# v's projection and the output projection change places in the batch loop of a graph-attention kernel

## The chip, the cores and the metric

The kernel runs on one core of one Trainium2 chip. The metric is the device time of one execution in microseconds. A core has five engines that run their own instruction queues and meet through semaphores: TensorE (PE, its weight loads shown as PEld), VectorE (DVE), ScalarE (ACT), GpSimd (POOL), and SyncE (SP), which here only issues DMAs. An engine carries out its queue in order, so whatever stands behind a waiting instruction waits too.

## The reference

For each of 32 graphs with 256 nodes and 512 features, with 16 heads of 32 features, in float32:

```python
h = jnp.maximum(_layernorm(x, axis=-1), 0.0)
q, k, v = h @ Wq.T, h @ Wk.T, h @ Wv.T            # split into 16 heads of 32
a = einsum('bhnd,bhmd->bhnm', q, k) * 512 ** -0.5 + (adj + adj)[:, None]
row_nonzero = jnp.any(a != 0, axis=-1, keepdims=True)
p = softmax(where(row_nonzero, a, -inf)); p = where(isnan(p), 0.0, p)
o = einsum('bhnm,bhmd->bhnd', p, v)               # heads joined again
out = x + o @ Wo.T
```

## The kernel before

**Precision.** Float32 products are made of float16 ones: every operand is split into a high and a low part (`*_hi`, `*_lo`), and three products (high-high, high-low, low-high) are added in PSUM. ScalarE evicts a PSUM bank into the high part, VectorE then takes the rest into the low part and frees the bank. Both have to be done before the bank is used again.

**Slots and steps.** One slot handles three batches at once: the batch before (`prev`), the current one (`cur`) and the next (`nxt`). A slot has 16 steps, one for each head of the current batch; `slot(t)` of each engine writes out by hand what it does in which step. There are 34 slots: `first`, `second`, 30 in the steady loop, `last` and `tail`. In a slot TensorE projects q, k and v of the next batch and the output of the batch before, computes the scores of four heads at a time (steps 0, 4, 8, 12), and multiplies probabilities by v (also in steps 0, 4, 8, 12, for the four heads of two groups earlier).

**Projections.** `JOBS` names eight jobs of two steps each: q01 in steps 0 and 1, q23, k01, k23, then o0 and o1 (steps 8 to 11), then v0 and v1 (12 to 15). Each job fills one of two PSUM banks, alternately; `pj_taken[0]` and `pj_taken[1]` count how often a bank was freed, `pj_full` how many jobs are done. So each job waits until the one two places before it has left the bank. q, k and v jobs are followed by an eviction on ScalarE one step later (`take_q`, `take_k`, `take_v`; v in steps 14 and 0) and the rest on VectorE another step later (`take_qk`, `take_v`; v in 15 and 1). The output jobs are followed only by `residual` on VectorE (steps 10 and 12, L759), which scales, adds x and writes the sum over x in SBUF. Job o0 waits for `o_split` (L953's group, in step 8): GpSimd must have split all four groups of o of the batch before, the last of them in its step 7.

**Softmax.** VectorE's `logit_rows` (L669) adds the adjacency to the scores and finds the row minima, two blocks of rows per head; ScalarE takes the exponential two steps ahead of its step number (L488) and rounds the head before that to float16 (L501); GpSimd's `split_probs` (L394) takes the rest; SyncE issues the DMA transpose of that head one step later (L325), and TensorE multiplies with v when four heads have landed. VectorE's `invert` (steps 3, 7, 11, 15: a reciprocal, L686, and `some`, L687) gives the factors that GpSimd spreads (`norm`, L403, one step later) and TensorE turns (L999). VectorE's `take_norm` copies them (L706), `take_o` (L698) applies them, and GpSimd's `take_o` (L413 and L416, in steps 3, 7, 11, 15) splits the result. `some` reads two SBUF tensors; L669, L698, L721, L731 and L759 read one from PSUM and one from SBUF.

**Next batches.** VectorE takes the statistics of the batch after next in steps 0 and 2 (L574, L580, L582, L583), GpSimd normalises in step 3 (L368, L374 `xn`), TensorE turns h in steps 5 and 9 (L836). `test_rows` (step 14 of VectorE, L745 and L753) tests rows for zeros. x has a ring of five buffers; its load is issued in SyncE's step 2, the two halves of the output are stored in SyncE's steps 12 and 14, each after its residual, and the load of a buffer waits for the store from it.

**Wo.** The weights are split at the start; Wo's four chunks are turned in steps 7 to 10 of the second slot (`WO_STEP`, L874), when that slot has no output projection and the two banks are free. v0 and v1 of that slot wait for two of the chunks to be taken from the banks.

Of the kernel before, what the change touches and what calls it, by code (L numbers as in the profile page):

```python
# [8 lines left out]
ALU = mybir.AluOpType  # L9
# [25 lines left out]

JOBS = ("q01", "q23", "k01", "k23", "o0", "o1", "v0", "v1")
NJ = len(JOBS)


class Slot:  # L40
# [23 lines left out]
    def uses(self, j):  # L64

        return self.prev if j in (4, 5) else self.nxt


def emit(nc, x_d, adj_d, wq_d, wk_d, wv_d, wo_d, out_d):
# [5 lines left out]
    with ctx:  # L75
# [162 lines left out]
        def full_step(t, j):  # L238
            if t.nxt:
                return 3 if j == 3 and not t.prev else 1  # L240
            return {4: 5, 5: 3}[j]

        def taken_step(t, j):
            if t.nxt:
                return 2 if j in (2, 3) and not t.prev else 1
            return 4

        def bank_free_at(t, j):

            return pj_taken_at(t, j) - (1 if t.nxt else 3)  # L250

# [5 lines left out]
        def group(t, c):  # L257

            d = c // NC
            return (d, c % NC) if t.has(d) else (None, None)  # L260

        def later(t, d):
# [12 lines left out]

        WO_STEP = 7

# [25 lines left out]
        def _(sp):  # L303
# [24 lines left out]
            def slot(t):  # L328
                for s in range(H):
                    turn(t, s - 1)  # L330
                    if s == 0 and later(t, 2):

                        need(sp, adj_scaled, t.batch(1))
                        need(sp, adj_checked, t.batch(1))
                        sp.dma_start(adj_raw[:, t.par(2)], av[t.batch(2)]).then_inc(adj_in[t.par(2)], 16)
                    if s == 2 and later(t, 3):
                        b = t.batch(3)

                        need(sp, out_done[b % 2 ^ 1], 16 * NU * ((b - X_RING) // 2 + 1))
                        sp.dma_start(xs[:, b % X_RING], xv[b]).then_inc(x_in[b % X_RING], 16)  # L340
                    if s in (12, 14) and t.prev:

                        u = (s - 12) // 2
                        sp.wait_ge(pj_taken[u], pj_taken_at(t, 4 + u))
                        sp.dma_start(ov[t.batch(-1)][:, u, :], xs[:, t.batch(-1) % X_RING, u, :])\
                          .then_inc(out_done[t.par(-1)], 16)

# [7 lines left out]
        def _(pool):  # L355
# [51 lines left out]
            def take_o(t, d, c):  # L407

                pool.wait_ge(o_ready, NC * t.batch(d) + (c + 1))
                if c == 0:  # L410

                    pool.wait_ge(pj_full, NJ * t.batch(d) + 6)
                g.tensor_scalar(o_hi[:, t.par(d), c, :], o_norm[:, c % 2], 1.0, 1.0, ALU.mult, ALU.mult)\  # L413
                 .then_inc(o_hi_ready, 1)
                pool.wait_ge(o_hi_ready, NC * t.batch(d) + (c + 1))
                g.tensor_tensor(o_lo[:, t.par(d), c, :], o_norm[:, c % 2], o_hi[:, t.par(d), c, :],  # L416
                                ALU.subtract).then_inc(o_split, 1)
# [30 lines left out]
        def _(act):  # L448
# [73 lines left out]
            def take_v(t, d, u):  # L522

                act.wait_ge(pj_full, NJ * t.batch(d) + (7 + u))
                if u == 0:

                    need(act, pv_done, NC * t.batch(d - 1))
                a.activation(v_hi[:, t.par(d), u, :], ps[:, PJ_BANK + u, :], ACT.Copy, scale=DOWN)\  # L528
                 .then_inc(v_hi_ready, 1)
                if Y_C:  # L530
                    a.activation(v_y[:, t.par(d), u],
                                 ps[:, PJ_BANK + u, :].rearrange("p (c j d) -> p c j d", c=NC, j=HC)[:, :, YJ, :],
                                 ACT.Copy, scale=DOWN).then_inc(v_hi_ready, 1)

            def slot(t):
                for s in range(H):
                    if s == 0 and t.cur:
                        take_v(t, 0, 1)
                    if s == 14 and t.nxt:
                        take_v(t, 1, 0)  # L540
                    if t.nxt:
# [19 lines left out]
        def _(dve):  # L561
# [156 lines left out]
            def take_v(t, d, u):  # L718
# [3 lines left out]
                                       in1=v_hi[:, t.par(d), u, :], op0=ALU.mult, op1=ALU.subtract)\  # L722
                 .then_inc(pj_taken[u], 1)

# [30 lines left out]

            def residual(t, u):

                dve.wait_ge(pj_full, pj_full_at(t, 4 + u))
                v.scalar_tensor_tensor(out=xs[:, t.batch(-1) % X_RING, u, :], in0=ps[:, PJ_BANK + u, :],  # L759
                                       scalar=out_scale[:, 0:1], in1=xs[:, t.batch(-1) % X_RING, u, :],  # L760
                                       op0=ALU.mult, op1=ALU.add).then_inc(pj_taken[u], taken_step(t, 4 + u))

            LOGITS = {1: (0, 3), 2: (3, 6), 3: (6, 8)}

            def slot(t):
                for s in range(H):
# [6 lines left out]
                    if s % 4 == 2 and s >= 10 and t.cur:  # L773
                        take_o(t, 0, s // 4 - 2)
                    if t.prev and s in (10, 12):
                        residual(t, (s - 10) // 2)
                    if s == 1 and t.cur:
                        take_v(t, 0, 1)
                    if s == 15 and t.nxt:
                        take_v(t, 1, 0)  # L780
                    if s in (3, 5, 7, 9) and t.nxt:
# [14 lines left out]
                    if t.nxt:  # L796
                        if s == (10 if t.first else 4):
                            check_adj(t)
                        if s == 14:
                            test_rows(t)  # L800
# [24 lines left out]
        def _(pe):  # L825
# [39 lines left out]
            def turn_last_weights(kc):  # L865

                if kc < 2:

                    pe.wait_ge(pj_taken[kc], bank_free_at(second, 4 + kc))
                else:  # L870
# [21 lines left out]
            def part_products(t, j):  # L892
# [3 lines left out]
                if j < 4:  # L896
                    w = j // 2
                    for c in range(2):
                        steps = [(kc, a, b) for kc in range(NC) for a, b in THREE]
                        for i, (kc, a, b) in enumerate(steps):  # L900
                            fs = P * (2 * g + c)
                            out.append((ps[:, PJ_BANK + g, N * c:N * c + N], W[a][:, w, kc, fs:fs + P],
                                        HT[b][:, t.par(1), kc, :], i == 0, i == len(steps) - 1))
                elif j < 6:
                    steps = [(c, a, b) for c in range(NC) for a, b in THREE]
# [10 lines left out]
            def project_last(t, d, c):  # L916
# [3 lines left out]
                for u in range(NU):  # L920
                    if c == 0:

                        pe.wait_ge(pj_taken[u], bank_free_at(tail, 4 + u))
                    for k, (a, b) in enumerate(THREE):
                        m = mm(ps[:, PJ_BANK + u, :], O[a][:, t.par(d), c, P * u:P * u + P], W[b][:, 3, c, :],
                               start=(c == 0 and k == 0), stop=(c == NC - 1 and k == len(THREE) - 1))
                    if c == NC - 1:
                        m.then_inc(pj_full, full_step(tail, 4 + u))

            def project(t, s):  # L930

                j, part = s // 2, s % 2
                if not t.uses(j) or t is tail:
                    return
                if part == 0:

                    need(pe, pj_taken[j % 2], bank_free_at(t, j))
                    if j == 0:

                        pe.wait_ge(aux_taken, aux_after("h", t.batch(1), 1))  # L940
                    if j == 4:

                        pe.wait_ge(o_split, NC * t.batch(0))
                    if t.first and j in (0, 2, 6):

                        pe.wait_ge(wt_taken, NC * (1 + {0: 0, 2: 1, 6: 2}[j]))
                    if t is second and j in (6, 7):

                        pe.wait_ge(wt_taken, NC * 3 + NC - 7 + j)
                products = part_products(t, j)  # L950
# [52 lines left out]
            def values(t, d, c):  # L1003
# [8 lines left out]
                if c == 0:  # L1012

                    for u in range(NU):
                        pe.wait_ge(pj_taken[u], (NJ // 2) * (t.batch(d) + 1))
                for mh in range(NU):
# [85 lines left out]
```

## Time and profile before

| | |
|---|---|
| median of 3 runs | 1030.49 us (1030.35 to 1031.45) |
| the profiled execution | 1030.06 us |
| its span on the core | 1028.3 us |
| mean granted TensorE clock | 0.983 |
| busy: PE, ACT, POOL, DVE | 95%, 90%, 86%, 86% of the span |
| DMA engines' share, queue 1 | 93.8% |
| chain that ended last, by engine | PE 40%, POOL 31%, ACT 19%, issue 6%, DVE 2% |

The page gives for each group of instructions its busy time, the mean duration of one, and the idle time of its engine just before them with what ended it. The chain of work is followed back from the last instruction to what released each step. Durations of neighbours on an engine overlap a little in the records, so times in the text are taken from start to start where two starts are to be had. All times of rows are us from the start of the span, of the profiled execution.

### The profile page before, as it was taken

Reading aid. Unit: us, or ns where it says so; the run is one execution under the profiler, and the core shown is the slowest. Engines: PE = TensorE matmul, PEld = TensorE weight load, DVE = VectorE, ACT = ScalarE, POOL = GpSimd, SP = SyncE. Lnnn points to the kernel's source line nnn. Section 1 sums busy time; section 2 is a strip of 40 time slices with the busy share of each in tenths; the row PEclk is TensorE's granted clock in tenths of the full one; section 3 lists DMA queues with packets and bytes.
Section 4 is the critical chain, followed back from the end, with each engine's and each line's share of the span. In section 5 each row is a group of like instructions: output and inputs, shape, how many; then the busy total and the mean of one; then the engine's idle time right before and its main releaser. Section 6 shows DMA issues by size and latency. Waiting matters only on the chain.

```text
span 1028.3 us, 34209 instructions
## 1 busy us (share of the span) xinstructions
PE 980.3 (95%) x11596; PEld 662.6 (64%) x11596; DVE 880.8 (86%) x3218; ACT 930.1 (90%) x3025; POOL 886.2 (86%) x1064
## 2 busy tenths in 40 slices
PE   6779999999999999999999999999999999999976
PEld 5556666666666666676666666666666666666733
DVE  6788998888899888899888889988888998888873
ACT  3499999999999999999999999999999999999992
POOL 1189998999999999999999999999999999999894
PEclk9899999999999999999999999999999999999978
DMA  6089999999999899999999999999999998999995
GB/s 245 11 144 173 190 185 170 191 181 187 187 188 194 174 187 175 190 186 189 188 176 185 182 186 183 192 172 189 179 186 190 187 196 173 187 175 167 164 173 128
DMA packets 569582, 182.62 MB, mean 178 GB/s; under 512 B 542784, under 2 KB 550976, under 8 KB 569408
## 3 DMA queue, kind: packets, MB, share of 16 engines
q1 hardware_dynamic: 569408, 180.43, 93.8%
q8 instruction: 93, 1.52, 0.6%
q14 instruction: 81, 0.66, 0.2%
HBM read 29.36 MB, written 16.78 MB: 45 GB/s over the span
## 4 chain that ended last, share of the span: by engine, by line
PE 40%; POOL 31%; ACT 19%; issue 6%; DVE 2%; DMA 1%; ACTq 0%; SPq 0%; POOLq 0%; DVEq 0%
PE ps L953 26%; POOL p L394 17%; ACT probs L488 13%; PE ps L1025 5%; PE ps L971 5%; POOL xn L374 4%; POOL o_lo L416 4%; ACT p L501 4%; POOL o_hi L413 2%; POOL rstd L368 2%; PE ps L836 2%; ACT v_hi L528 2%; POOL norm L403 2%; DVE w_max L589 1%; PE ps L999 1%
## 5 line engine op out<-in xcount | busy, mean ns | idle before, releaser
L394 POOL TENSOR_TENSOR p<-probs,p 128x512 f16<-128x512 f32 x512 | 588.7, 1160 | 86.9 <-ACT p L501 82.7
L488 ACT ACTIVATE probs<-logits,row_min 128x256 f32<-128x256 f32 x1024 | 508.7, 502 | 2.6 <-DVE row_min L669 2.6
L669 DVE CUSTOM_DVE_ANT_0 logits<-ps,adj_s,sigma 128x256 f32<-128x256 f32 x1024 | 441.3, 476 | 20.2 <-PE ps L971 13.2
L501 ACT ACTIVATE p<-probs 128x512 f16<-128x512 f32 x512 | 318.6, 622 | 0.0
L953 PE MATMUL ps<-ht_hi,w_hi 128*128 128x256 f16 x1024 | 279.7, 273 | 1.2 <-DVE q_lo L731 1.2
L953 PE MATMUL ps<-ht_hi,w_lo 128*128 128x256 f16 x1024 | 279.3, 273 | 0.0
L953 PE MATMUL ps<-ht_lo,w_hi 128*128 128x256 f16 x1024 | 279.3, 273 | 0.0
L488 ACT ACTIVATION_READ_ACCUMULATOR probs<-logits,row_min 128x1 f32 x1024 | 200.2, 196 | 0.0
L953 PEld LDWEIGHTS ps<-ht_hi,w_hi 128*128 128x128 f16 x1024 | 100.2, 98 | 21.7 <-issue 6.8
L953 PEld LDWEIGHTS ps<-ht_lo,w_hi 128*128 128x128 f16 x1024 | 100.3, 98 | 14.6
L953 PEld LDWEIGHTS ps<-ht_hi,w_lo 128*128 128x128 f16 x1024 | 100.3, 98 | 11.7
L953 PE MATMUL ps<-w_hi,o_hi 128*128 128x512 f16 x248 | 94.4, 381 | 12.5 <-POOL o_lo L416 12.5
L1025 PE MATMUL ps<-pt,v_hi 128*32 128x256 f16 x2048 | 97.6, 278 | 5.7 <-DMA pt<-p 3.2
L953 PE MATMUL ps<-w_hi,ht_hi 128*128 128x512 f16 x256 | 98.1, 383 | 1.8 <-DVE w_lo L629 1.8
L953 PE MATMUL ps<-w_hi,ht_lo 128*128 128x512 f16 x256 | 98.0, 383 | 0.0
L953 PE MATMUL ps<-w_lo,ht_hi 128*128 128x512 f16 x256 | 98.0, 383 | 0.0
L416 POOL TENSOR_TENSOR o_lo<-o_norm,o_hi 128x256 f16<-128x256 f32 x128 | 85.9, 671 | 10.7
L953 PE MATMUL ps<-w_hi,o_lo 128*128 128x512 f16 x248 | 94.5, 381 | 0.0
L953 PE MATMUL ps<-w_lo,o_hi 128*128 128x512 f16 x248 | 94.4, 381 | 0.0
L731 DVE SCALAR_TENSOR_TENSOR k_lo<-ps,k_hi 128x512 f16<-128x512 f32 x64 | 44.2, 690 | 51.9 <-ACT k_hi L518 51.9
L669 DVE DVE_READ_ACCUMULATOR2_ANT row_min<- 128x1 f32 x1024 | 82.3, 80 | 0.0
L403 POOL TENSOR_TENSOR norm<-recip,some 128x256 f32<-128x256 f32 x128 | 78.7, 615 | 0.8 <-DVE some L687 0.8
(84 smaller groups left out, 1659.1 us busy)
## 6 DMA issues: line engine op xcount, KB each, us to landing
xs<-in_x SPq DMA_DIRECT2D x32, 512.0 KB, 4.5
out<-xs SPq DMA_DIRECT2D x64, 256.0 KB, 2.6
adj_raw<-in_adj SPq DMA_DIRECT2D x32, 256.0 KB, 4.0
pt<-p SPq DMA_TRANSPOSE x512, 3.4
w_nat<-in_L_gnn_Wq SPq DMA_DIRECT2D x1, 1024.0 KB, 6.4
w_nat<-in_L_gnn_Wk SPq DMA_DIRECT2D x1, 1024.0 KB, 9.1
w_nat<-in_L_gnn_Wv SPq DMA_DIRECT2D x1, 1024.0 KB, 11.3
w_nat<-in_L_gnn_Wo SPq DMA_DIRECT2D x1, 1024.0 KB, 13.2
```

Of the source, the lines that this page charges most:

```text
L368: g.tensor_tensor(rstd[:], var_s[:], minus_half[:], ALU.pow).then_inc(rstd_ready, 1)
L374: g.tensor_scalar(xn[:, u, :], xs[:, t.batch(d) % X_RING, u, :], neg_mean[:, u:u + 1], rstd[:, u:u + 1], ALU.add, ALU.mult).then_inc(xn_re ...
L394: g.tensor_tensor(p16[:, c % 2, k, 1], probs[:, h % 4].rearrange("p u n -> p (u n)"), p16[:, c % 2, k, 0], ALU.subtract).then_inc(p_split, 1)
L403: g.tensor_tensor(norm[:, c % 2].rearrange("p u (j d) -> p u j d", j=HC), recip[:].unsqueeze(3).broadcast_to(wide), some[:].unsqueeze(3).b ...
L416: g.tensor_tensor(o_lo[:, t.par(d), c, :], o_norm[:, c % 2], o_hi[:, t.par(d), c, :], ALU.subtract).then_inc(o_split, 1)
L488: e = a.activation(probs[:, h % 4, u, :], logits[:, h % 4, u, :], ACT.Exp, bias=row_min[:, t.par(d), u, h:h + 1], scale=-1.0, accum_out=ro ...
L501: a.activation(p16[:, c % 2, k, 0], probs[:, h % 4].rearrange("p u n -> p (u n)"), ACT.Copy)\
L669: v.tensor_tensor_reduce(out=logits[:, h % 4, u, :], in0=ps[:, S_BANK + h % HC, N * u:N * u + N], in1=adj_s[:, t.par(d), u, :], scale=sigm ...
L731: v.scalar_tensor_tensor(out=lo[:, t.par(1), 2 * g:2 * g + 2, :].rearrange("p c n -> p (c n)"), in0=ps[:, PJ_BANK + g, :], scalar=-DOWN if ...
L953: m = mm(o, l, r, start=start, stop=stop)
L971: m = mm(ps[:, S_BANK + j, N * u:N * u + N], Q[x][HD * j:HD * j + HD, t.par(d), c, P * u:P * u + P], K[y][HD * j:HD * j + HD, t.par(d), c, ...
L1025: m = mm(o, (v_hi, v_lo)[a][:, t.par(d), mh, HD * h:HD * h + HD], pt16[:, c % 2, j, 2 * NU * b + mh:2 * NU * b + mh + NU + 1:NU, :], start ...
```

## The change

v's projection goes to steps 8 to 11 and the output projection to steps 12 to 15. The first slot, where q, k and v of batch 0 are made, and the two last ones, where no next batch is left, keep their order (`job_at`). With the jobs move:

- ScalarE's eviction of v: from steps 14 and 0 to steps 10 and 12; VectorE's rest of v: from 15 and 1 to 11 and 13.
- VectorE's residuals: from steps 10 and 12 to step 14 and to step 0 of the next slot; they now stand behind `take_norm` and `take_o` and before the logits and statistics of their step.
- `test_rows`: from step 14 to step 15, behind the logits of that step.
- SyncE's stores: from steps 12 and 14 to step 15 and step 1 of the next slot; the load of x from step 2 to step 6.
- The turn of Wo in the second slot: from steps 7 to 10 to steps 11 to 14.
- The counts that the waits on `pj_full` and `pj_taken` compare with.

```diff
@@ -33,7 +33,7 @@
 
-JOBS = ("q01", "q23", "k01", "k23", "o0", "o1", "v0", "v1")
+JOBS = ("q01", "q23", "k01", "k23", "v0", "v1", "o0", "o1")
 NJ = len(JOBS)
@@ -63,7 +63,7 @@
 
-        return self.prev if j in (4, 5) else self.nxt
+        return self.prev if j in (6, 7) else self.nxt
 
@@ -237,17 +237,17 @@
             if t.nxt:
-                return 3 if j == 3 and not t.prev else 1
-            return {4: 5, 5: 3}[j]
+                return 3 if j == 5 and not t.prev else 1
+            return {6: 7, 7: 1}[j]
 
...
             if t.nxt:
-                return 2 if j in (2, 3) and not t.prev else 1
+                return 2 if j in (4, 5) and t.batch(1) < 2 else 1
             return 4
...
 
-            return pj_taken_at(t, j) - (1 if t.nxt else 3)
+            return pj_taken_at(t, j) - (1 if t.nxt else 4)
 
@@ -259,6 +259,16 @@
 
+        def residuals(t, s):
+
+            if not t.nxt and s in (10, 12):
+                return [(t.batch(-1), (s - 10) // 2)]
+            if t.nxt and t.prev and s == 14:
+                return [(t.batch(-1), 0)]
+            if t is not tail and t.batch(-2) >= 0 and s == 0:
+                return [(t.batch(-2), 1)]
+            return []
+
         def later(t, d):
@@ -273,7 +283,18 @@
 
-        WO_STEP = 7
+        WO_STEP = 11
+
+        def job_at(t, s):
+
+            if t.first and s >= H // 2:
+                return s // 2 - 2 if s >= 12 else None
+            if not t.nxt:
+                return s // 2 + 2 if s in range(8, 12) else None
+            return s // 2
+
+        def v_steps(t):
+            return ((14, 16) if t.first else (10, 12))
 
@@ -333,17 +354,14 @@
                         sp.dma_start(adj_raw[:, t.par(2)], av[t.batch(2)]).then_inc(adj_in[t.par(2)], 16)
-                    if s == 2 and later(t, 3):
+                    if s == 6 and later(t, 3):
                         b = t.batch(3)
...
                         sp.dma_start(xs[:, b % X_RING], xv[b]).then_inc(x_in[b % X_RING], 16)
-                    if s in (12, 14) and t.prev:
-
-                        u = (s - 12) // 2
-                        sp.wait_ge(pj_taken[u], pj_taken_at(t, 4 + u))
-                        sp.dma_start(ov[t.batch(-1)][:, u, :], xs[:, t.batch(-1) % X_RING, u, :])\
-                          .then_inc(out_done[t.par(-1)], 16)
+                    for b, u in residuals(t, s - 1):
+                        sp.wait_ge(pj_taken[u], (NJ // 2) * (b + 3))
+                        sp.dma_start(ov[b][:, u, :], xs[:, b % X_RING, u, :]).then_inc(out_done[b % 2], 16)
 
@@ -409,7 +427,7 @@
 
-                    pool.wait_ge(pj_full, NJ * t.batch(d) + 6)
+                    pool.wait_ge(pj_full, NJ * t.batch(d) + NJ)
                 g.tensor_scalar(o_hi[:, t.par(d), c, :], o_norm[:, c % 2], 1.0, 1.0, ALU.mult, ALU.mult)\
@@ -521,7 +539,7 @@
 
-                act.wait_ge(pj_full, NJ * t.batch(d) + (7 + u))
+                act.wait_ge(pj_full, NJ * t.batch(d) + (5 + u))
                 if u == 0:
@@ -534,10 +552,10 @@
                 for s in range(H):
-                    if s == 0 and t.cur:
+                    if s == 0 and t is second:
                         take_v(t, 0, 1)
-                    if s == 14 and t.nxt:
-                        take_v(t, 1, 0)
+                    if s in v_steps(t) and t.nxt:
+                        take_v(t, 1, v_steps(t).index(s))
                     if t.nxt:
@@ -720,7 +738,7 @@
                                        in1=v_hi[:, t.par(d), u, :], op0=ALU.mult, op1=ALU.subtract)\
-                 .then_inc(pj_taken[u], 1)
+                 .then_inc(pj_taken[u], 2 if t.batch(d) < 2 else 1)
 
@@ -753,12 +771,13 @@
 
-            def residual(t, u):
-
-                dve.wait_ge(pj_full, pj_full_at(t, 4 + u))
-                v.scalar_tensor_tensor(out=xs[:, t.batch(-1) % X_RING, u, :], in0=ps[:, PJ_BANK + u, :],
-                                       scalar=out_scale[:, 0:1], in1=xs[:, t.batch(-1) % X_RING, u, :],
-                                       op0=ALU.mult, op1=ALU.add).then_inc(pj_taken[u], taken_step(t, 4 + u))
+            def residual(b, u):
+
+                dve.wait_ge(pj_full, NJ * (b + 2) + (7 + u))
+                v.scalar_tensor_tensor(out=xs[:, b % X_RING, u, :], in0=ps[:, PJ_BANK + u, :],
+                                       scalar=out_scale[:, 0:1], in1=xs[:, b % X_RING, u, :],
+                                       op0=ALU.mult, op1=ALU.add)\
+                 .then_inc(pj_taken[u], 4 if b >= NB - 2 else 1)
 
@@ -772,12 +791,12 @@
                         take_o(t, 0, s // 4 - 2)
-                    if t.prev and s in (10, 12):
-                        residual(t, (s - 10) // 2)
-                    if s == 1 and t.cur:
+                    for b, u in residuals(t, s):
+                        residual(b, u)
+                    if s == 1 and t is second:
                         take_v(t, 0, 1)
-                    if s == 15 and t.nxt:
-                        take_v(t, 1, 0)
+                    if s - 1 in v_steps(t) and t.nxt:
+                        take_v(t, 1, v_steps(t).index(s - 1))
                     if s in (3, 5, 7, 9) and t.nxt:
@@ -796,7 +815,7 @@
                             check_adj(t)
-                        if s == 14:
+                        if s == 15:
                             test_rows(t)
@@ -866,7 +885,7 @@
 
-                    pe.wait_ge(pj_taken[kc], bank_free_at(second, 4 + kc))
+                    pe.wait_ge(pj_taken[kc], bank_free_at(second, 6 + kc))
                 else:
@@ -901,7 +920,7 @@
                                         HT[b][:, t.par(1), kc, :], i == 0, i == len(steps) - 1))
-                elif j < 6:
+                elif j >= 6:
                     steps = [(c, a, b) for c in range(NC) for a, b in THREE]
@@ -920,17 +939,17 @@
 
-                        pe.wait_ge(pj_taken[u], bank_free_at(tail, 4 + u))
+                        pe.wait_ge(pj_taken[u], bank_free_at(tail, 6 + u))
                     for k, (a, b) in enumerate(THREE):
...
                     if c == NC - 1:
-                        m.then_inc(pj_full, full_step(tail, 4 + u))
+                        m.then_inc(pj_full, full_step(tail, 6 + u))
 
...
 
-                j, part = s // 2, s % 2
-                if not t.uses(j) or t is tail:
+                j, part = job_at(t, s), s % 2
+                if j is None or not t.uses(j) or t is tail:
                     return
@@ -938,15 +957,15 @@
                         pe.wait_ge(aux_taken, aux_after("h", t.batch(1), 1))
-                    if j == 4:
+                    if j == 6:
 
                         pe.wait_ge(o_split, NC * t.batch(0))
-                    if t.first and j in (0, 2, 6):
-
-                        pe.wait_ge(wt_taken, NC * (1 + {0: 0, 2: 1, 6: 2}[j]))
-                    if t is second and j in (6, 7):
-
-                        pe.wait_ge(wt_taken, NC * 3 + NC - 7 + j)
+                    if t.first and j in (0, 2, 4):
+
+                        pe.wait_ge(wt_taken, NC * (1 + {0: 0, 2: 1, 4: 2}[j]))
+                    if t.batch(1) == 2 and j in (0, 1):
+
+                        pe.wait_ge(wt_taken, NC * 3 + NC - 1 + j)
                 products = part_products(t, j)
@@ -1012,7 +1031,7 @@
                     for u in range(NU):
-                        pe.wait_ge(pj_taken[u], (NJ // 2) * (t.batch(d) + 1))
+                        pe.wait_ge(pj_taken[u], (NJ // 2) * t.batch(d) + 3)
                 for mh in range(NU):
...
                         o = ps[HD * j:HD * j + HD, PV_BANK, 0:N]

```

## Rows read from the trace of the kernel before

**Rows 1.** The chain that ended last, steady state: start us, us, what.

```profile
501.49 1.08 ACT probs L488 x4
...
519.11 1.46 PE ps L953 x6
```

**Rows 2.** Waits over the whole span: us in total, times, longest us.

```profile
PE ps L953 <- POOL o_lo L416: 12.5, 30, 2.3
```

**Rows 3.** The same of ten steady slots, 424.2 to 726.5 us.

```profile
ACT v_hi L528 <- PE ps L953: 12.0, 10, 1.2
...
PEld ps L836 <- POOL xn L374: 2.9, 10, 0.3
PEld ps L836 <- issue: 2.1, 10, 0.2
```

**Rows 4.** The chain near the end, where it stays on TensorE.

```profile
942.25 1.46 PE ps L953 x6
...
970.26 2.60 PE ps L953 x18
```

**Rows 5.** ScalarE in time: start us, us, line op out<-in xcount [idle before <-releaser].

```profile
485.74 0.38 ACT L518 ACTIVATE k_hi<-ps 128x256 f16<-128x256 f32 x1
...
499.16 0.62 ACT L501 ACTIVATE p<-probs 128x512 f16<-128x512 f32 x1
501.00 0.60 ACT L528 ACTIVATE v_hi<-ps 128x512 f16<-128x512 f32 x1 [1.21 <-PE ps L953]
```

**Rows 6.** TensorE in time, same columns.

```profile
488.90 0.38 PE L953 MATMUL ps<-w_hi,o_hi 128*128 128x512 f16 x1 [0.36 <-POOL o_lo L416]
...
500.58 0.38 PE L953 MATMUL ps<-w_hi,ht_lo 128*128 128x512 f16 x1
...
510.92 0.27 PE L953 MATMUL ps<-ht_hi,w_hi 128*128 128x256 f16 x1
...
512.33 0.29 PE L971 MATMUL ps<-k_hi,q_hi 32*128 32x256 f16 x4
```

**Rows 7.** GpSimd in time.

```profile
494.51 0.41 POOL L413 TENSOR_SCALAR o_hi<-o_norm 128x256 f16<-128x256 f32 x1
...
495.62 1.16 POOL L394 TENSOR_TENSOR p<-probs,p 128x512 f16<-128x512 f32 x1
...
510.46 1.16 POOL L394 TENSOR_TENSOR p<-probs,p 128x512 f16<-128x512 f32 x1
```

**Rows 8.** VectorE in time.

```profile
493.83 0.75 DVE L759 SCALAR_TENSOR_TENSOR xs<-ps,out_scale,xs 128x512 f32<-128x512 f32 x1 [1.02 <-PE ps L953]
494.50 0.48 DVE L669 CUSTOM_DVE_ANT_0 logits<-ps,adj_s,sigma 128x256 f32<-128x256 f32 x1
...
495.82 0.99 DVE L687 SCALAR_TENSOR_TENSOR some<-row_min,some_qk 128x8 f32<-128x8 f32 x1
...
500.68 0.47 DVE L669 CUSTOM_DVE_ANT_0 logits<-ps,adj_s,sigma 128x256 f32<-128x256 f32 x1
...
502.31 0.68 DVE L721 SCALAR_TENSOR_TENSOR v_lo<-ps,v_hi 128x512 f16<-128x512 f32 x1
...
503.02 0.12 DVE L687 SCALAR_TENSOR_TENSOR some<-row_min,some_qk 128x8 f32<-128x8 f32 x1
...
509.93 0.19 DVE L686 RECIPROCAL recip<-row_sum 128x8 f32<-128x8 f32 x1
```

**Rows 9.** VectorE and GpSimd in the last slot but one.

```profile
983.84 0.48 DVE L753 TENSOR_SCALAR some_qk<-some_qk 128x32 f32<-128x32 f32 x1
...
983.89 0.40 POOL L413 TENSOR_SCALAR o_hi<-o_norm 128x256 f16<-128x256 f32 x1
```

**Rows 10.** Line 583: duration ns min/median/max, first and last start.

```profile
L583 DVE TENSOR_SCALAR var_s<-mean_var x32: 153/155/163, 6.4 to 932.4; 128x2 f32<-128x2 f32 x32
```

**Rows 11.** DMA issues, page: count, us to landing.

```profile
pt<-p SPq DMA_TRANSPOSE x512, 3.4
```

**Rows 12.** TensorE in the second slot.

```profile
66.90 0.65 PE L874 MATMUL ps<-ident,w_nat 128*128 128x128 f32 x4 [1.77 <-DVE k_lo L731]
```

## The prediction

> **What bounds the kernel now.** I read the chain that ended last first. In steady state it repeats every 30.2 us: TensorE starts step 8 at 488.90 [rows 6] and again at 519.11; between them it passes to ScalarE in step 14 (501.49), then to GpSimd, and back to TensorE through GpSimd's last `o_lo` [rows 1]. So no engine alone sets the period: a loop over three engines does. Its joints are waits. TensorE waits for `o_lo` before the output projection 30 times, 12.5 us in all, 2.3 us of it once near the end [rows 2]; that leaves 10.2 us in 29 slots, 0.35 each. ScalarE waits 12.0 / 10 = 1.2 us a slot for v's projection; TensorE's turn of h in step 5 waits 0.29 us against 0.21 us for the same gap in step 9, so GpSimd's `xn` costs it 0.08 us a slot [rows 3]. VectorE waits 1.0 us for the output projection in step 10 (the 493.83 row of [rows 8]).
>
> **What TensorE needs by itself.** After 942.25 the chain stays on TensorE for a whole slot: step 8 starts at 942.25, and in the piece at 970.26 (18 matmuls, the first 12 of 256 columns, step 7's) the next step 8 starts 12 x 0.109 = 1.31 us later, at 971.57 [rows 4] (a matmul of 512 columns takes the array 0.216 us: 1.31 us for six in the chain; one of 256 half of it). That is 29.32 us, without one turn of h (about 0.49 us with its gap; the slot had one of the two). So TensorE alone takes 29.8 us, which is also 30.23 - 0.35 - 0.08. This is all that the change can win in the loop: 0.43 us a slot.
>
> **The change part by part.** *The wait on `o_lo`.* The output projection starts at step 12, some 7.5 us after step 8 (24 matmuls of 0.216 us are 5.2 us; scores, values, one turn of h and one of the norm are the rest). The last split of GpSimd ends before step 8's start, so it is covered by 7 us: 29 x 0.35 = -10.2 us. If the cover were gone, the old 0.35 would be back. The 0.08 for `xn` goes too where TensorE comes later to step 5, as it will: -2.3 us.
>
> *ScalarE.* v's two evictions move from steps 14 and 0 to 10 and 12. ScalarE starts step 10 at 499.16 less three heads of 1.5 us and two exponentials of 0.49, 493.7, when TensorE's step 9 has just ended (0.2 us ahead of the residual at 493.83 [rows 5, 8]); so the 1.2 us of waiting vanish there, but its next take of q at step 2 waits for TensorE as before. The count of its instructions is the same; the slack is only moved: 0. It has a side effect. From the k eviction of step 6 (485.74) to the end of head 14's rounding (499.16 + 0.52) are 13.94 us [rows 5]; two v evictions of 0.49 us (501.00 to the next at 501.49 [rows 1, 5]) now lie inside: 14.92. TensorE's step 13 ends at 500.58 + 0.22 = 500.80 [rows 6], 15.06 after that k eviction, 14.70 without the 0.36 us of waiting. Call that end zero. Then GpSimd gets head 14 at +0.22, starts it 0.17 us later, takes 1.15 us, and then 1.11 us for `o_hi` and `o_lo` (494.51 to 495.62 [rows 7]): `o_lo` ends at +2.65, and head 15 follows at once.
>
> *VectorE.* This is the part that gives gain back. In the old slot VectorE runs from the logits of step 14 (500.68) to the end of q_lo (509.93) with no wait that the trace names: 9.25 us [rows 8]. Now: out go two v_lo of 0.6 us (0.68 less the 0.08 by which neighbours overlap), in comes residual u=1 of 0.67 us (493.83 to 494.50), and ahead stands residual u=0, which starts 0.2 us after zero and takes 0.67. End of q_lo: 0.2 + 0.67 + 9.25 - 1.2 + 0.67 = +9.6. TensorE wants its bank for k at 510.92, which is +10.12 [rows 6]. Cover: 0.5 us, less 0.1 for the hand-over. Two rows eat it. `some` (L687) takes 0.12 us at 503.02, when GpSimd is idle, and 0.99 us at 495.82, when GpSimd's split runs from 495.62 to 496.78: it ends with GpSimd's instruction [rows 7, 8]. In step 15 it comes at 0.2 + 0.67 + 1.2 + 0.12 = +2.2, inside `o_lo` (to +2.65): +0.4 us. And `test_rows`, moved behind step 15's logits, ends in L753, normally 0.18 us; at 983.84 it took 0.48, to the end of GpSimd's `o_hi` [rows 9]. It now comes at +3.7, less than 0.1 us before head 15's split ends (+3.8). If it gets in there, it costs nothing; if it misses, `norm` holds it to +4.4, 0.5 us. I take the row it is nearest to, 983.84, which missed a boundary by as little. So q_lo ends 0.4 to 0.9 us late: at +10.0 or +10.5, against +10.0 allowed: a stall of 0 to 0.45.
>
> *The scores of step 4* have a second claim: `some` of step 3 now comes at +10.1 or later instead of before GpSimd's split of head 3 (which starts as now at 510.46, +9.66, since ScalarE is held by q in step 2 as now [rows 7]) and waits to +10.8; two logits of 0.4 us end at +11.65, and with 0.14 us of hand-over the scores start at +11.8 instead of at 512.33, +11.53 [rows 6]: 0.26 us. The two stalls lie on the same TensorE time, so the larger counts. I take 0.3 us a slot, ends 0 and 0.5: 29 x 0.3 = +8.7 us.
>
> A rule that weighs on this: the Trainium skill (GPSIMD Engine Reference, Specifications) says that GpSimd shares its SBUF interfaces with VectorE and contends with VectorE instructions that have two SBUF inputs or run in a two-port mode. By it `var_s` (L583), a float32 operation from SBUF to SBUF, would be held as well, up to one GpSimd `o_lo` more in step 2. The trace speaks against that: L583 never took over 0.163 us in 32 times [rows 10]. By the row this costs nothing, by the page up to 0.6 us a slot.
>
> *Residuals and bank hand-over.* o0 in steps 12 and 13 needs v_lo u=0 of VectorE's step 11. ScalarE's eviction ends 0.5 us after TensorE's step 9, v_lo 1.3 us after; step 12 starts 2.8 us after: covered. The count of bank waits is the same; u=1 of the output no longer needs ScalarE at all: 0.
>
> *SyncE's queue.* Both stores move from steps 12 and 14 to 15 and 1, the load of x from 2 to 6. Each issue takes 0.6 us there and transposes wait behind it. The store at step 1 waits for a residual that ends at about +6, when head 1's split is not done (+6.6): nothing waits longer than now. A transpose lands 3.4 us after issue [rows 11], and values read head 15's some 8 us after its split. Cost 0; if the cover were gone, the issue time, 0.6 us a slot. x has 9 steps, some 17 us, from its load to its statistics.
>
> *The second slot.* Turning Wo moves by four steps with the free steps of TensorE. It meets the same round trip as now, TensorE to ScalarE to VectorE (1.77 us of waiting once at 66.90 [rows 12]), then ahead of v, now ahead of q of the next slot: 0, ends -2 and +2. *The end.* The two last slots keep the order. ScalarE no longer has v's eviction and its wait of 1.2 us in front of the last heads, but the waits for logits behind residual u=0 take most of it: -0.6, ends 0 and -1.3.
>
> **Sum.** 1030.06 (profiled execution) - 10.2 - 2.3 + 8.7 - 0.6 = 1025.7. The median shown is 1030.49, 0.43 above, so 1026.1; I give 1026.0.
>
> **The rivals.** *Whole gain (20%).* The stall on VectorE doesn't come: `some` gets its turn early, or VectorE regains time elsewhere. For it: the cover is missed by tenths of a microsecond, and my hand-overs may be long. Against it: from step 10's residual to step 3 VectorE has no idle time in which to regain any. 1026.1 - 8.7 = 1017.4.
>
> *Gain eaten whole (20%).* L753 misses and the hand-overs are slower than I read: a stall of 0.43, or the transposes, 3.4 us each and one every 1.9 us [rows 11], so always two in flight, are a bound of their own at 30.2 us. Against the latter: in the slot from 942.25 they kept up with a period of 29.3 us [rows 4], though without a load of x. About 1030.5 less the end's 0.6: 1030.
>
> *Slower (13%).* Place: `some` of step 15. If GpSimd ended `o_lo` before VectorE asks at +2.2, head 15's split of 1.15 us would already run, and `some` would wait 0.85 us as at 495.82, not 0.4. The stall becomes 0.3 + 0.45 = 0.75, over the 0.43 won: 29 x 0.32 = +9.3, 1030.5 - 0.6 + 9.3 = 1039. It decides from GpSimd being 0.45 us earlier than I reckon, that is if ScalarE is.
>
> *Forecast (47%)*, 1026, own range 1021.5 to 1029.5.
>
> **How the numbers follow.** About 0.2%, 2 us, is what a measurement can tell from no change. Faster: 20 + most (42) of the forecast = 0.62. Same: 20 + 5 = 0.25. Slower: 0.13. The range leaves out the far part of the slower case and the lowest end of the whole gain: 1017.0 to 1034.0.
>
> **What would show it.** Right: no wait of TensorE for `o_lo` outside the end; the wait of ScalarE for v gone and one of about 1.2 us for q in step 2 in its place; `some` of step 15 at 0.5 us or more instead of 0.12; a wait of TensorE in step 4 on q_lo or on the last row minimum. A chain that stays on TensorE for whole slots means the whole gain. L753 at 0.18 or above 0.5 tells whether it met the boundary. Wrong altogether: a TensorE wait in another step, transposes that land much later than 3.4 us, or a granted clock below full speed in the steady slots.

## The result, and the profile after

| | before | changed |
|---|---|---|
| median | 1030.62 us (4 executions, 1030.35 to 1031.45) | 1014.29 us (4 executions, 1011.3 to 1015.38) |
| profiled execution, its span | 1030.06, 1028.3 | 1015.38, 1013.6 |
| period of a steady slot | 30.22 us | 29.69 us |
| chain that ended last | PE 40%, POOL 31%, ACT 19% | PE 74%, DVE 17%, POOL 3%, ACT 3% |

The ratio is 0.9843, 95% interval 0.9825 to 0.9861. The change is faster by 1.6% or 16.3 us, more than three times the 4.5 us that I forecast, and lies below my range.

The period comes from the starts of the row test's matmuls in step 13, one for each of the 32 batches. From the third to the 31st are 28 periods: 107.88 to 954.16 before, 108.99 to 940.38 after (the last slot with a row test turns no h and is shorter, 28.56 us in both). The profiled executions differ by 14.7 us. The 28 periods shrink by 14.9 us; up to the third row test the changed kernel took 1.1 us more, behind the 31st 0.9 us less.

To see where TensorE loses time within a slot, I took the distances between the starts of its groups of matmuls and subtracted what the same group takes where nothing holds it. There are three such gaps in a steady slot before, and one after:

```
gap ahead of                                before   changed
output projection, step 8 (now step 12)       0.52      none
turn of h, step 5                             0.08      none
values, step 12                               0.11      none
scores, step 4                                none      0.18
period                                       30.22     29.69
period less its gaps                         29.51     29.51
```

The waits of some ten steady slots (424 to 727 us) of the changed kernel, where [rows 3] had v's eviction and the turn of h (columns: us in total, times, longest):

```profile
POOL p L412 <- ACT p L519: 15.1, 40, 0.5
...
ACT q_hi L529 <- PE ps L972: 8.8, 10, 0.9
...
PEld ps L990 <- DVE row_min L687: 3.8, 10, 0.4
DVE xs L777 <- PE ps L972: 3.5, 10, 0.4
...
PEld ps L855 <- POOL xn L392: 2.1, 10, 0.2
```

TensorE's wait for `o_lo` is gone from the list, ScalarE's wait for v has become one for q of 0.9 us, and the scores (L990) wait for a row minimum. The chain that ended last says the same. It stays on TensorE from step 4 to the next slot's step 0, and then runs on VectorE (start us, us, what; the pieces left out are VectorE's too, or "issue" of at most 0.3 us):

```profile
499.47 0.77 PE ps L990 x24
500.24 0.85 PE ps L1044 x24
501.09 0.03 DVEq L195
501.12 0.17 DVE stats L592
501.29 0.38 DVE logits L687
...
504.98 0.19 DVE recip L704
505.17 0.66 DVE some L705
505.83 0.40 DVE logits L687
506.23 0.40 DVE logits L687
506.63 0.02 DVE row_min L687
506.65 0.05 issue
506.69 0.83 PE ps L990 x24
```

VectorE in time, from residual u=0 in step 14 on; TensorE's step 13 ends at 494.99, which is the zero of my sum:

```profile
495.19 0.75 DVE L777 SCALAR_TENSOR_TENSOR xs<-ps,out_scale,xs 128x512 f32<-128x512 f32 x1 [0.34 <-PE ps L972]
...
497.18 0.11 DVE L705 SCALAR_TENSOR_TENSOR some<-row_min,some_qk 128x8 f32<-128x8 f32 x1
...
498.35 0.75 DVE L771 TENSOR_SCALAR some_qk<-some_qk 128x32 f32<-128x32 f32 x1
...
504.23 0.17 DVE L600 TENSOR_SCALAR neg_mean<-mean_var 128x2 f32<-128x2 f32 x1
504.30 0.16 DVE L601 TENSOR_SCALAR var_s<-mean_var 128x2 f32<-128x2 f32 x1
504.37 0.68 DVE L749 SCALAR_TENSOR_TENSOR q_lo<-ps,q_hi 128x512 f16<-128x512 f32 x1
504.98 0.19 DVE L704 RECIPROCAL recip<-row_sum 128x8 f32<-128x8 f32 x1
505.08 0.74 DVE L705 SCALAR_TENSOR_TENSOR some<-row_min,some_qk 128x8 f32<-128x8 f32 x1
```

And GpSimd beside it:

```profile
496.80 0.40 POOL L431 TENSOR_SCALAR o_hi<-o_norm 128x256 f16<-128x256 f32 x1
497.28 0.68 POOL L434 TENSOR_TENSOR o_lo<-o_norm,o_hi 128x256 f16<-128x256 f32 x1
497.91 1.16 POOL L412 TENSOR_TENSOR p<-probs,p 128x512 f16<-128x512 f32 x1
...
504.65 1.16 POOL L412 TENSOR_TENSOR p<-probs,p 128x512 f16<-128x512 f32 x1 [0.52 <-ACT p L519]
```

The split of q ends at 504.98, +9.99, in time for the k bank. `some` of step 3 asks at 505.08, when GpSimd's split of head 3 has run since 504.65, and ends at 505.82 with it. Two logits later, 506.69 instead of 506.52, the scores start: 0.18 us late with the rounding of the starts. `some` of step 15 slipped in between `o_hi` (to 497.20) and `o_lo` (from 497.28) and took 0.11 us. L771, the old L753, was held from 498.35 to the end of head 15's split at 499.07, 0.75 us instead of 0.18.

### The profile page after: what moved, and what is told of

Read it like the earlier page. It is cut to its first block, busy times and chain, and to the rows that moved or that the text cites. A ratio compares the mean times of both kernels' runs of the same rounds, so it can differ in the third digit from the quotient of the medians.

```text
span 1013.6 us, 34208 instructions
## 1 busy us (share of the span) xinstructions
PE 974.8 (96%) x11596; PEld 662.7 (65%) x11596; DVE 870.4 (86%) x3218; ACT 927.0 (91%) x3025; POOL 885.2 (87%) x1064
## 4 chain that ended last, share of the span: by engine, by line
PE 74%; DVE 17%; POOL 3%; ACT 3%; issue 2%; DMA 1%; SPq 0%; DVEq 0%; ACTq 0%; POOLq 0%
PE ps L972 48%; PE ps L1044 10%; PE ps L990 9%; DVE logits L687 9%; PE ps L855 4%; PE ps L1018 2%; POOL p L412 2%; DVE some L705 2%; ACT probs L506 1%; DVE o_norm L716 1%; DVE w_max L607 1%; DVE q_lo L749 1%; DMA w_nat<-in_L_gnn_Wq 1%; ACT p L519 1%; PE ps L1055 1%
## 5 line engine op out<-in xcount | busy, mean ns | idle before, releaser
L519 ACT ACTIVATE p<-probs 128x512 f16<-128x512 f32 x512 | 322.0, 629 | 0.0
L506 ACT ACTIVATION_READ_ACCUMULATOR probs<-logits,row_min 128x1 f32 x1024 | 207.0, 202 | 0.0
L739 DVE SCALAR_TENSOR_TENSOR v_lo<-ps,v_hi 128x512 f16<-128x512 f32 x64 | 44.2, 691 | 43.8 <-ACT v_hi L546 43.8
```

The costliest lines, as they stand in the source:

```text
L506: e = a.activation(probs[:, h % 4, u, :], logits[:, h % 4, u, :], ACT.Exp, bias=row_min[:, t.par(d), u, h:h + 1], scale=-1.0, accum_out=ro ...
L519: a.activation(p16[:, c % 2, k, 0], probs[:, h % 4].rearrange("p u n -> p (u n)"), ACT.Copy)\
L739: v.scalar_tensor_tensor(out=v_lo[:, t.par(d), u, :], in0=ps[:, PJ_BANK + u, :], scalar=DOWN, in1=v_hi[:, t.par(d), u, :], op0=ALU.mult, o ...
```

## The experiments

Theory 1: the gain is TensorE's waits themselves, measured by starts; what VectorE gives back is the one operation with two SBUF inputs in step 3. The rivals: that v's earlier evictions are the gain, that the idle column sizes the wait, that VectorE's load as such is the stall, that SyncE's moves were needed.

**The wait alone, in the kernel before**

```diff
                     if j == 4:
-                        pe.wait_ge(o_split, NC * t.batch(0))
+                        pe.wait_ge(o_split, NC * t.batch(0) - 2)
...
+                if part == 1 and j == 4:
+                    pe.wait_ge(o_split, NC * t.batch(0))
                 products = part_products(t, j)
```

> The kernel before, with one edit: the output projection's first half (step 8), which reads only the first two of the four groups of o, waits for these two alone, and the wait for all four stands ahead of its second half (step 9). No step is moved. Theory 1 (what the change won is the wait on o_lo itself, and it was worth 0.52 us a slot by starts of matmuls, not the 0.36 of the idle column): that wait is gone, the two small ones stay (0.07 before the turn of h, 0.11 before the values of step 12); the period falls from 30.22 to about 29.7 us, the time to about 1015. Theory 2 (the order of v's evictions, that is ScalarE's wait in step 14, is what was won): the loop stays within 0.1 us of 30.2, time 1027 to 1031. Theory 3 (the idle column is right): 30.22 - 0.36 = 29.86 and 1019 to 1020.

Measured: 1009.24 us (1006.68 to 1009.59), ratio to before 0.9793 (0.9778 to 0.9808), 6 us less than I expected. The period is 29.59 us: the gap of 0.52 is gone, that of 0.08 ahead of the turn of h is left, and the 0.11 ahead of step 12's values went as well, which I had not expected. Without moving a step this kernel is 4 to 5 us faster than the changed one (1014.29, and 1012.90 when it ran again). So the order of v's evictions was not what was won (theory 2): ScalarE still waits 0.6 us a slot for v here. And 0.36 us a slot, the idle column, is too little (theory 3): the period fell by 0.63, of which 0.11 is the gap of step 12 and 0.52 the wait. Its chain is TensorE in 90% of the span:

```profile
PE 90%; DVE 3%; POOL 3%; ACT 2%; DMA 1%; issue 1%; SPq 0%; ACTq 0%; POOLq 0%; DVEq 0%
```

The gap ahead of step 12's values went because a hold of `some` in step 11 got shorter. Before, `some` asks at 495.82, when GpSimd's split has run since 495.62, and takes 0.99 us [rows 7, 8]; `norm_t`, which the values wait for, follows late (kernel before, VectorE, then TensorE's values):

```profile
498.14 0.41 DVE L706 COPY norm_t<-ps 128x256 f32<-128x256 f32 x1
```

```profile
498.69 0.42 PE L1025 MATMUL ps<-pt,v_hi 128*32 128x256 f16 x8
```

In this experiment `some` asks while GpSimd's `o_lo` runs, ahead of that split, and is held only to the end of `o_lo` (VectorE, then GpSimd):

```profile
483.94 0.75 DVE L759 SCALAR_TENSOR_TENSOR xs<-ps,out_scale,xs 128x512 f32<-128x512 f32 x1 [0.75 <-PE ps L955]
...
485.93 0.38 DVE L687 SCALAR_TENSOR_TENSOR some<-row_min,some_qk 128x8 f32<-128x8 f32 x1
...
487.65 0.41 DVE L706 COPY norm_t<-ps 128x256 f32<-128x256 f32 x1
```

```profile
485.62 0.67 POOL L416 TENSOR_TENSOR o_lo<-o_norm,o_hi 128x256 f16<-128x256 f32 x1
486.25 1.16 POOL L394 TENSOR_TENSOR p<-probs,p 128x512 f16<-128x512 f32 x1
```

The scores of step 12 start at 497.83 before and at 487.94 here. Counted from there, the residual of step 10 starts 4.0 us earlier and `some` 2.0 us earlier in both kernels; the hold is 0.6 us shorter here, and `norm_t` ends 0.12 us after the start of the scores instead of 0.72.

**The logits first in step 3**

```diff
-                    if s % 4 == 3 and t.cur:
+                    if s % 4 == 3 and s != 3 and t.cur:
                         invert(t, 0, s // 4)
                     if s % 4:
                         logit_rows(t, (s + 3) // 4, *LOGITS[s % 4])
+                    if s == 3 and t.cur:
+                        invert(t, 0, s // 4)
```

> The changed kernel, with VectorE's step 3 in another order: the two logits of the step first, then reciprocal and the two-input operation. Theory 1 (that operation, held 0.74 us until GpSimd's split of head 3 ends, is what delays the row minima for which TensorE's scores of step 4 wait 0.18 us): the wait is gone, the period falls from 29.69 to 29.52 us, 28 to 29 slots by 0.17 = 5 us, time about 1009.5. Rival (the wait is for the k bank or for the length of VectorE's work, whatever its order): the period stays at 29.65 to 29.7 and the time within 1 us of the changed kernel.

Measured: 1009.46 us (1009.1 to 1009.86), ratio 0.9799 (0.9783 to 0.9816). The gap ahead of the scores is gone, `some` of step 3 takes 0.11 us:

```profile
502.01 0.47 DVE L687 CUSTOM_DVE_ANT_0 logits<-ps,adj_s,sigma 128x256 f32<-128x256 f32 x1
502.41 0.48 DVE L687 CUSTOM_DVE_ANT_0 logits<-ps,adj_s,sigma 128x256 f32<-128x256 f32 x1
...
502.94 0.11 DVE L705 SCALAR_TENSOR_TENSOR some<-row_min,some_qk 128x8 f32<-128x8 f32 x1
```

But the period is 29.61, not 29.52: with TensorE 0.18 us earlier, the old 0.08 ahead of the turn of h is back. The steady slots give only 2.3 us of the 4.8 between the medians, and of the 3.4 to the second measurement of the changed kernel (1012.90). Between the profiled executions, 1015.38 and 1009.86, the other parts are 1.9 us up to the third row test and 1.3 us behind the 31st. The 1.9 is not the edit's: against the other profiled execution of the changed kernel it is 0.2. The mechanism is shown, the size only in part.

**One more operation in step 0, and half of one**

```diff
+                    if s == 0 and t.prev and later(t, 2):
+                        v.bn_stats(spare[:], w_nat[:, 3, 0, :])
                     if later(t, 2):
```

The second kernel has `w_nat[:, 3, 0, 0:256]` in its place.

> The changed kernel, with one more statistics operation of 512 elements (0.60 us, its result is not used) in VectorE's step 0, behind the residual. Theory 1 (VectorE runs without idle time from step 14's residual to the rest of q, which ended at +9.99 us after TensorE's step 13 against +10.12 when the k projection wants the bank): q's rest ends at +10.6, k starts 0.5 to 0.6 us late, the period is 29.52 + 0.55 = 30.07, 0.38 over the changed kernel, time about 1025. Rival (there is idle time or slack in that stretch that the trace doesn't name): less than 0.15 us a slot, under 1019.

> The changed kernel with one more statistics operation of 256 elements (about 0.33 us) in VectorE's step 0; the one of 512 elements (0.60 us) cost 1.28 us a slot. Theory 1 (of those, 0.9 us were neg_mean held until GpSimd's split of head 3 ended; with half the size neg_mean asks 0.1 us before that split starts and isn't held): q's rest ends at about +10.3, period 29.7 to 29.85 us, time 1014 to 1019. Rival (the cost is proportional): 29.69 + 0.6 = 30.3 us, time 1031 or more.

Measured, one execution each: 1047.78 us with a period of 30.97, and 1015.61 us with 29.85. So 0.60 us of work cost 1.28 us a slot, and 0.33 us cost 0.15. The first was far over the 0.38 that I expected, and its trace says why (VectorE, then GpSimd):

```profile
519.44 0.24 DVE L599 BATCH_NORM_AGGREGATE mean_var<-stats 128x2 f32<-128x6 f32 x2
519.72 1.03 DVE L601 TENSOR_SCALAR neg_mean<-mean_var 128x2 f32<-128x2 f32 x1
520.66 0.15 DVE L602 TENSOR_SCALAR var_s<-mean_var 128x2 f32<-128x2 f32 x1
520.73 0.68 DVE L750 SCALAR_TENSOR_TENSOR q_lo<-ps,q_hi 128x512 f16<-128x512 f32 x1
```

```profile
518.89 0.67 POOL L435 TENSOR_TENSOR o_lo<-o_norm,o_hi 128x256 f16<-128x256 f32 x1
519.57 1.16 POOL L413 TENSOR_TENSOR p<-probs,p 128x512 f16<-128x512 f32 x1
```

`neg_mean`, 0.17 us elsewhere, asks at 519.72, just after GpSimd's split has begun at 519.57, and is held to its end at 520.73. In the half-size kernel it asks at 503.41, before the split at 503.50, and takes 0.17 us. That is the step in the cost: 0.87 us for being 0.15 us late instead of 0.09 us early. The rival of a proportional cost (30.3 us) is out, and so is hidden idle time on VectorE.

**The load of x back in step 2**

```diff
-                    if s == 6 and later(t, 3):
+                    if s == 2 and later(t, 3):
```

> The changed kernel, with the load of x back in SyncE's step 2, where it has to wait for the store issued in step 1 (3.3 us to landing). Theory 1: the transposes of heads 2 and 3 go out up to 3 us later, but values read them some 8 us after their split, so the cover holds: period 29.69 to 29.75, time within 1.5 us of the changed kernel. Rival (SyncE's queue is tight, the moves of its steps were needed): values wait for transposes in step 8, 0.5 us or more a slot, 1028 or more.

Measured: 1017.61 us, one execution, 3.3 us above the changed kernel's median where I had allowed 1.5. Most steady slots have the period of 29.69, but the 28 together take 2.6 us more than in the changed kernel. In five of them the values of step 8 wait 0.10 to 0.86 us, 2.2 us in all, the longest in a slot of 30.56:

```profile
277.54 0.43 PE L1044 MATMUL ps<-pt,v_hi 128*32 128x256 f16 x8 [0.79 <-DVE k_lo L749]
```

The releaser named there is not it: `k_lo` of the next batch only counts up the semaphore on which v's rest, done in the slot before, is counted. These values also read the transposes of heads 0 to 3. The transpose of head 3 was issued at 270.07, behind the load of x at 268.27, and landed at 277.23, 7.2 us later. In all five slots the values start 0.31 us after that landing. In the two profiled executions of the changed kernel they start 2.9 to 5.9 us after it, and no slot waits. So the rival was right in kind: the place of x's load keeps the transposes clear. Its size was far off, 0.1 us a slot on average for 0.5, and the load's place is no part of what the change won.

**The changed kernel beside the others, and the ends**

> The changed kernel itself, once more, beside the following ones. Its four executions lay between 1011.3 and 1015.4. All theories: period 29.69 us and a median of 1012.5 to 1015; what differs between executions lies ahead of the third slot and behind the last steady one, where the granted clock falls, not in the period.

> The changed kernel with the split wait alone. Theory 1: period 29.69 as in the changed kernel, time 2 to 4 us under the changed kernel run beside it (about 1011), all of it behind the last steady slot. Rival: within 1 us of the changed kernel.

> The changed kernel with two edits: VectorE's logits first in step 3, and the wait on o_lo split over the two halves of the output projection. In steady slots the output projection no longer waits, so only the last slots can gain from the second. Theory 1 (the second edit shortens TensorE's wait of 2 to 3 us in the last slot, and its clock doesn't fall there): period 29.61, time about 1006.5, 3 us under the kernel with the first edit alone (1009.5). Rival (the end is set by other engines): 1009 to 1010.

The second of these is the first experiment's edit made in the changed kernel (job 6 for job 4), the third has the logits first as well. Measured, with before at 1029.83 us beside them:

```
                         median    executions             ratio to before, 95%      period
changed, again          1012.90    1010.69 to 1013.55     0.9825, 0.9808 to 0.9841  29.69
split wait              1010.12    1008.86 to 1010.65     0.9800, 0.9783 to 0.9816  29.69
split wait, logits 1st  1007.65    1006.89 to 1011.05     0.9784, 0.9764 to 0.9804  29.60
```

The split wait leaves the period alone and gives 2.8 us, so that comes from the ends: in the last slot the output projection still waits for `o_lo`. There the changed kernel (the first row) runs 5 us at half the clock; the first experiment (the second row) does not around the same work (us, then busy time of PE, PEld, DVE, ACT and POOL, then the granted clock, DMA share, GB/s):

```profile
980.40:985.40 5.00, 1.71 (x5) 0.72 (x6) 2.74 (x14) 5.00 (x19) 4.92 (x7) 0.50 1.03 200
```

```profile
974.70:979.70 5.00, 3.43 (x56) 1.71 (x48) 4.24 (x20) 5.00 (x17) 4.92 (x6) 0.91 0.84 160
```

In the first of the two rows TensorE waited 3.1 us for `o_lo` and was busy 1.71 of 5 us, and its clock stood at 1.2 GHz; with 3.43 of 5 us it was at 2.4 GHz for most. The first experiment has a stretch at the lower clock too, earlier (0.72 from 970 to 975 us). Behind the 31st row test the changed kernel takes 73.2 us at a mean granted clock of 0.88 (73.0 at 0.88 in its second profile), the same kernel with the split wait 69.0 at 0.95, and the first experiment 70.1 at 0.95. These runs don't part what the wait cost by itself from what the clock cost. Nor is the end the same in every execution: the profiled one with both edits took 72.0 us there, at 0.90.

The kernel with both edits is 1.8 us below the one with the logits first alone, where I had expected 3, and 1.6 us below the first experiment, which is within what their executions differ; no claim is made between these two. The first row test starts anywhere from 44.9 to 47.9 us in these profiles, in kernels with the same start. Between the two profiled executions of the changed kernel that is 1.7 of the 1.9 us by which they differ; the other executions left no trace.

## Why the prediction was wrong, step by step

**What bounds the kernel, and that the wait goes:** right. The loop over three engines opened, TensorE bounds most of the slot (VectorE the stretch up to step 4), and the wait is gone in every steady slot.

**The size of the wait on `o_lo`: the main miss.** I took the idle column, 0.36 us [rows 2, 6]. It counts from the modelled end of the matmul before, which starts at 488.27 and is shown as 0.27 us long, to 488.54. But neighbours of that form start 0.109 us apart, so the next could have started at 488.38. From there to 488.90 are 0.52 us, and the first experiment took just that off the period. I had used the distance of starts for everything else. I gave the wait 10.2 us; it was worth 28 x 0.52 = 14.6, so the miss is 4.4 us.

**What TensorE needs by itself:** 29.8 us was wrong, and hid the miss above, since I took the agreement of two sums as proof. The piece at 970.26 [rows 4] does not begin with step 7: that step's first matmul is at 970.10 in the time view, so step 8 starts at 971.40, not 971.57. And the slot still held the wait of step 12. 971.40 - 942.25 + 0.49 - 0.12 = 29.52, which is the measured period less its gaps within 0.01. With it the whole gain would have been 0.71 us a slot, not 0.43, and its rival 29 x 0.28 = 8 us lower, about 1009 instead of 1017.4; my lower end stood on that cap.

**A wait I had not seen.** Before step 12's values TensorE loses 0.11 us. It is in no row of the waits: the time view has it as the start of the values at 498.69, 0.86 us after the scores instead of 0.76. `norm_t` of that step, which the values wait for, ended at 498.55, late behind `some` of step 11, which GpSimd's split held for 0.99 us: the very row that I had taken the price of a hold from [rows 8]. I never asked what it cost where it stood. In the first experiment the residual of step 10 is in its old place and the gap is gone with the shorter hold; in the changed kernel `some` of step 11 takes 0.12 us. I had put this term at nothing; it is 28 x 0.11 = 3.1 us.

**The stall that VectorE gives back:** the place was right, the scores of step 4, held by `some` of step 3 behind the split of head 3. The end of q's rest was forecast at +10.0 or +10.5 and came at +9.99, the scores at +11.8 and came at +11.70. I took 0.3 us a slot, 8.7 us in all; measured are 0.18, 28 x 0.18 = 5.0: a miss of 3.7 us. Of the two rows below, L753 cost what I had set for a miss (0.57 us for 0.5), but not as I had it: it asked at +3.36, well inside head 15's split, and was held by the split itself, not past its end by `norm`. That the price came out is luck. `some` of step 15, for which I had 0.4 us and named 0.5 as a sign, was not held, as a gap of 0.08 us between two GpSimd instructions let it in.

The wait on `o_lo`, the wait of step 12 and the stall add to 11.2 us (4.4 + 3.1 + 3.7). My sum for the profiled execution was 1025.7; less 11.2, with the 1.1 us that the start took more and the 0.3 that the end gave beyond my 0.6, it is 1015.3, and that execution took 1015.38. (I had counted 29 slots; 28 periods got shorter.) The median, 1014.29, is 1.1 us lower; where the executions without a trace saved that, the runs don't tell.

**`xn`:** right, 0.08 gone, and it came back where the stall went. **ScalarE's slack:** right, 0.9 us at q for the 1.2 at v. **Banks, SyncE, stores:** right, no wait; a store lands in 3.3 us for 2.6, a transpose in 3.5 for 3.4 [rows 11]. **The second slot:** from the first row test to the third it takes 61.1 us for 61.9, within my -2 to +2. **The end:** -0.9 for -0.6.

**The page against the row.** I set a rule of the Trainium skill (GPSIMD Engine Reference, Specifications: contention with VectorE operations in a two-port mode) aside because L583 never took over 0.163 us [rows 10]. The result was right here, the reason not. In the kernel before, `neg_mean` and `var_s` came in the last 0.2 us of GpSimd's split (VectorE, then GpSimd):

```profile
509.14 0.20 DVE L582 TENSOR_SCALAR neg_mean<-mean_var 128x2 f32<-128x2 f32 x1
509.26 0.15 DVE L583 TENSOR_SCALAR var_s<-mean_var 128x2 f32<-128x2 f32 x1
```

```profile
508.16 1.16 POOL L394 TENSOR_TENSOR p<-probs,p 128x512 f16<-128x512 f32 x1 [0.35 <-ACT p L501]
```

A row that meets only the end of the other engine's instruction can't show a long hold; `neg_mean` just ahead of it took 0.20 us for 0.17. With 0.6 us more ahead of it, `neg_mean` asked 0.15 us behind the start of a split and was held for 0.87 us. That agrees with the page if this operation ran in such a mode, which no trace shows. The slower rival had this mechanism with the wrong operation and place.

## What to carry to other kernels

Size a wait of TensorE by the starts of its matmuls, from the one before to the one after, less their usual distance; the idle column counts from a modelled end and showed 0.36 us for 0.52. Before a step is moved to cover a wait, look at what it reads: the first half of the projection needed only two of four groups, and splitting the wait gave more than moving eight steps. A wait that goes shifts the engines against each other and can take or bring another: look at every hold again. On VectorE, a small operation that can be held by GpSimd has a price that jumps: ask for the gap between its start and the start of GpSimd's next instruction, not for its mean.

## What the runs showed that I had not expected

- 0.60 us of work on VectorE cost 1.28 us a slot, 0.33 us cost 0.15. The difference is one operation of 0.17 us that came 0.15 us after instead of 0.09 us before a GpSimd instruction of 1.16 us.
- An operation of VectorE got in through 0.08 us between two GpSimd instructions (497.20 to 497.28).
- A wait of 0.52 us taken away also took one of 0.11 us, at another place in the slot: `some` of step 11 asked as early as before, but no longer just behind the start of GpSimd's split.
- The end of the kernel: behind the 31st row test the changed kernel took 73.2 us at a mean granted clock of 0.88, and 69.0 us at 0.95 with the wait on `o_lo` split.
